# Attention and a gated feed-forward block in one kernel: the end of the program rebuilt, the order of TensorE's work written anew

## The reference

```python
q = (xn @ wq + bq)  # 16 heads of 16;  k, v: 2 groups of 16, each shared by 8 heads
q, k = rotary(q) * 16**-0.5, rotary(k)
attn = softmax(q k^T * 16**-0.5)            # per head, 1024 x 1024
x + (attn v) @ wo + bo + fwht(silu(xn @ W1.T) * (xn @ W3.T)) @ W2.T
```

## Time and profile before

| | us |
|---|---|
| three runs: lowest, median, highest | 1078.07, 1078.76, 1084.82 |
| the profiled execution: its time | 1075.6 |
| the profiled execution: span | 1073.8 |
| PE busy | 1014.3 (94%) |
| DVE busy | 771.2 (72%) |
| ACT busy | 707.5 (66%) |
| POOL busy | 347.2 (32%) |

### The profile page before, as it was taken

How to read it: one execution, slowest core, us unless ns; L and a number is a source line. 1 busy time by engine, 2 the same in 40 slices (tenths; PEclk the granted TensorE clock), 3 DMA queues, 4 the chain that set the end, 5 groups by cost and what they waited for, 6 DMA issues and landing times.

```text
span 1073.8 us, 19578 instructions
## 1 busy us (share of the span) xinstructions
PE 1014.3 (94%) x7604; PEld 549.6 (51%) x7604; DVE 771.2 (72%) x934; ACT 707.5 (66%) x1336; POOL 347.2 (32%) x300
## 2 busy tenths in 40 slices
PE   4889999999999999999999999999999999999997
PEld 3554445545554555545554455545555454644454
DVE  5996688677776778767786777767776778776723
ACT  4256677657765777657776577667775678566873
POOL 5262722073312634054310735126320224012300
PEclk9998999999999999999999999999999999999999
DMA  8762155212052253402242250521123131510001
GB/s 234 177 172 75 53 137 104 74 57 86 17 117 78 76 136 66 100 21 84 64 103 74 97 126 18 117 64 51 51 62 71 33 83 33 111 32 6 12 8 50
DMA packets 64941, 84.03 MB, mean 78 GB/s; under 512 B 19960, under 2 KB 34168, under 8 KB 64848
## 3 DMA queue, kind: packets, MB, share of 16 engines
q1 hardware_dynamic: 63296, 80.74, 29.1%
q10 hardware_dynamic: 1552, 2.03, 0.7%
HBM read 54.97 MB, written 22.51 MB: 72 GB/s over the span
## 4 chain that ended last, share of the span: by engine, by line
PE 66%; DVE 17%; ACT 5%; issue 4%; DMA 4%; SPq 3%; POOL 2%; DVEq 0%; ACTq 0%; POOLq 0%
PE ps L1501 16%; PE ps L1558 14%; PE ps L1545 13%; DVE negpart L1295 11%; PE ps L1456 9%; PE ps L1513 8%; PE ps L1467 3%; DVE hid L1267 3%; PE ps L1434 3%; ACT work L1079 2%; DMA qk_parts<-hid 1%; DMA xn<-in_x 1%; SPq L776 1%; SPq L784 1%; DMA recip_rows<-dens 1%
## 5 line engine op out<-in xcount | busy, mean ns | idle before, releaser
L1295 DVE TENSOR_REDUCE negpart<-ps 128x2 f32<-128x1024 f32 x512 | 619.0, 1224 | 235.7 <-PE ps L1456 234.8
L1079 ACT ACTIVATE work<-ps 128x512 f32<-128x512 f32 x1024 | 560.0, 603 | 262.3 <-PE ps L1545 256.9
L1558 PE MATMUL ps<-work,vb 128*32 128x512 f32 x2048 | 274.6, 609 | 5.8 <-ACT osum L1090 5.0
L1545 PE MATMUL ps<-qh,kb 50*128 50x512 f32 x1024 | 265.1, 450 | 10.3 <-ACT work L1079 7.4
L1456 PE MATMUL ps<-kb,qh 48*128 48x512 f32 x1024 | 226.8, 433 | 9.6 <-DVE negpart L1295 5.3
L1545 PEld LDWEIGHTS ps<-qh,kb 50*128 50x128 f32 x1024 | 123.4, 185 | 212.3 <-ACT work L1079 159.0
L1501 PE MATMUL ps<-xf,w_p 64*128 64x512 f32 x1536 | 218.3, 400 | 7.4 <-DVE negpart L1295 1.4
L1501 PEld LDWEIGHTS ps<-xf,w_p 64*128 64x128 f32 x1536 | 143.6, 185 | 49.7 <-DVE hid L1267 16.3
L933 POOL TENSOR_TENSOR hid_p<-hid,hid_p 128x512 fp32r<-128x512 f32 x64 | 82.2, 1286 | 203.1 <-ACT hid_p L1068 203.1
L1456 PEld LDWEIGHTS ps<-kb,qh 48*128 48x128 f32 x1024 | 98.1, 185 | 82.7 <-DVE negpart L1295 48.4
L1513 PEld LDWEIGHTS ps<-w2t_p,hid_p 64*128 64x128 f32 x1536 | 107.7, 185 | 34.2 <-DVE negpart L1295 27.1
(11 more groups left out here) (125 smaller groups left out, 484.6 us busy)
## 6 DMA issues: line engine op xcount, KB each, us to landing
xf<-xn_parts SPq DMA_DIRECT2D x32, 512.0 KB, 8.5
qh<-qk_parts SPq DMA_DIRECT2D x192, 64.0 KB, 2.3
xn_parts<-xt SPq DMA_DIRECT2D x14, 512.0 KB, 3.5
qh<-mturned SPq DMA_DIRECT2D x256, 2.0 KB
y<-in_x SPq DMA_DIRECT2D x8, 512.0 KB, 4.8
attnt<-osum SPq DMA_DIRECT2D x124, 32.0 KB, 2.0
recips<-recip_rows SPq DMA_DIRECT2D x120, 32.0 KB, 1.8
xn<-in_x SPq DMA_DIRECT2D x7, 512.0 KB, 5.0
```

The lines of the kernel that those rows point to most:

```text
L1079: nc.scalar.activation(prob[(ITSTEPS * i + j) % NPROB][:, h, :], ps[:, 4 + u % 3, :], ACT.Exp, scale=SCALE).then_inc(exp_done, 1)
L1295: nc.vector.tensor_reduce(negpart[a][:, f, :, h, t, e], two(slot), AX.X, ALU.max, negate=True).then_inc(ring_free[slot], 1)
L1545: pe.matmul(ps[:, 4 + u % 3, :], kb[i % 2][rows, kt * P:(kt + 1) * P], qh[2 * a + f][rows, h, :], start=True, stop=True).then_inc(s2_done, 1)
L1558: m = pe.matmul(ps[VW * h:VW * (h + 1), 7, :], vb[b % 2][g][:, kt, :], prob[(ITSTEPS * i + j) % NPROB][:, h, :], start=(kt == 0), stop=(kt ...
```

## The change

1. **The end.** The last iteration's output projection of half 0 moves from the closing into period 15 (kind `WOz`). To make room, the down products go one period sooner (11 to 14) and the last up product from period 10 to 9; VectorE's reciprocals of half 0 go from period 13 to 12.
2. **The closing.** VectorE turns the last sums straight from PSUM in blocks of 32 x 32, in two halves of 256 columns; in the turned layout each query's row sum stands beside its 16 values, so 8 reciprocals per partition do; it multiplies and turns back. Heads 4 to 7 then stand spread, 16 of each 32 partitions, so their output weights are loaded into `wo_last`, spread the same way with zeros between (a memset on GpSimd in iteration 6 and four DMAs on SyncE). TensorE adds the two parts of half 1 up in PSUM: first four matmuls over 64 partitions for heads 0 to 3, then four with `wo_last`. ScalarE's last copy, `select`, `chosen` and the wide reciprocals go.
3. **The orders.** On TensorE the kinds DN, WO, QK, None, WOx, QKx, UPxo, Nos and Not get another order, and WOo takes that of WO. On ScalarE most kinds get another order: copies of up products and projections come before an exponential that stood ahead of them, and where `osum` is saved the copy moves. UP and XT keep TensorE's order.

```diff
-    return range(4, 12) if i + 2 < NBLK else (1, 2, 3, 5, 6, 7, 8, 10)
+    return range(4, 12) if i + 2 < NBLK else (1, 2, 3, 5, 6, 7, 8, 10 if i + 1 < NIT else 9)
+def down_at(i):
+    return range(12, 16) if i + 1 < NIT else range(11, 15)
...
-    if p >= 12:
-        return ("DN", i, p - 12)
+    if i + 1 == NIT and p == PERIODS - 1:
+        return ("WO", i, 0)
+    if p in down_at(i):
+        return ("DN", i, down_at(i).index(p))
...
 # kind DN, TensorE
             sums_before()
+            scores(1)
             own(0)
-            scores(1)
             first(1)
...
-        elif kind == "WO":
+        elif kind in ("WO", "WOo"):
             scores(0)
             first(1)
+            scores(1)
             own(0)
-            scores(1)
             scores(2)
             first(1)
             own(1, 2, 3)
+            scores(3)
             first(1)
             sums_before()
             first(0)
             sums(i, 2 * p)
-            scores(3)
...
 # kind QK, TensorE
             own(1, 2, 3)
             first(1)
+            scores(3)
             sums(i, 2 * p)
-            scores(3)
             extra()
...
 # kind None, TensorE
             first(0)
+            sums(i, 2 * p)
             first(1)
             scores(3)
-            sums(i, 2 * p)
...
+        elif kind == "WOx":
+            scores(0)
+            first(1)
+            own(0, 1)
+            first(1)
+            own(2, 3)
+            scores(1)
+            first(1)
+            sums_before()
+            sums(i, 2 * p)
+            first(0)
+            scores(2)
             extra()
             scores(3)
...
-        elif kind == "WOo":
-            first(0)
-            sums_before()
-            first(0)
-            first(1)
-            scores(0)
-            scores(1)
-            own(0, 1, 2, 3)
-            scores(2)
-            sums(i, 2 * p)
-            first(1)
-            scores(3)
...
-        elif kind == "DNz":
+        elif kind == "WOz":
             scores(0)
             scores(1)
+            sums_before()
             scores(2)
-            own(0)
+            own(0, 1)
             scores(3)
-            own(1, 2)
-            sums_before()
+            own(2, 3)
             sums(i, 2 * p)
-            own(3)
...
 # SyncE, iteration i, ahead of move_sums(i, 1)
+                if i == NIT - 2:
+                    sp.wait_ge(wo_zero, 1)
+                    for h in range(QUAD):
+                        at = (NG - 1) * P + (QUAD + h) * HD
+                        sp.dma_start(wo_last[VW * h:VW * h + HD, :], wo[at:at + HD, :]).then_inc(wo_last_in, 16)
...
 # ScalarE, kind UP
                         gate(i, up_at(i).index(p))
-                        exponentials(i, j, 5, 6)
                         linear(i, up_at(i).index(p))
-                        exponentials(i, j, 6, 8)
+                        exponentials(i, j, 5, 8)
 # ScalarE, kind QK
                         exponentials(i, j, 0, 5)
                         projected(i + 2, 0)
-                        exponentials(i, j, 5, 6)
                         projected(i + 2, 1)
-                        exponentials(i, j, 6, 8)
+                        exponentials(i, j, 5, 7)
                         projected(i + 2, 2)
+                        exponentials(i, j, 7, 8)
 # ScalarE, kind WOo
-                        exponentials(i, j, 0, 5)
+                        exponentials(i, j, 0, 7)
+                        hidden_before(i, p)
                         save_finished(i, p)
-                        exponentials(i, j, 5, 8)
-                        hidden_before(i, p)
+                        exponentials(i, j, 7, 8)
...
 # VectorE, the closing
+            dve.wait_ge(pv_done, ITSTEPS * NIT)
+            for n, cols in enumerate(halves):
+                nc.vector.transpose(last_sums[:, cols], ps[:, 7, cols]).then_inc(last_turned, 1)
             for n in range(2):
-                cols = slice(n * 2 * P, (n + 1) * 2 * P)
-                dve.wait_ge(last_turned, 1)
-                nc.vector.reciprocal(last[GRP:P, cols], ps[GRP:P, 5, cols]).then_inc(last_recip, 1)
-                dve.wait_ge(last_turned, 2)
-                dve.wait_ge(last_recip, n + 2)
-                nc.vector.tensor_tensor(attnt[GRP:P, 1, cols], ps[GRP:P, 4, cols], last[GRP:P, cols],
-                                        ALU.mult).then_inc(last_norm, 1)
-            projected_sums(NIT - 1, 0)
+                dve.wait_ge(last_turned, n + 1)
+                nc.vector.reciprocal(shares[n], blocks[n][:, :, HD]).then_inc(last_step, 1)
             for n in range(2):
-                at = y[:, (NBLK - 1) % 2, 2 * n:2 * n + 2, :].rearrange("p t d -> p (t d)")
-                dve.wait_ge(*filled(("WO", NIT - 1, 1), n + 1))
-                nc.vector.tensor_tensor(at, at, two(0)[:, n, :], ALU.add).then_inc(ring_free[0], 1)
+                dve.wait_ge(last_step, n + 1)
+                nc.vector.tensor_tensor(blocks[n][:, :, 0:HD], blocks[n][:, :, 0:HD],
+                                        shares[n].unsqueeze(2).broadcast_to([P, 2 * P // VW, HD]), ALU.mult).then_inc(last_step, 1)
+            for n, cols in enumerate(halves):
+                dve.wait_ge(last_step, n + 3)
+                nc.vector.transpose(last_attn[:, cols], last_sums[:, cols]).then_inc(last_norm, 1)
+            for n in range(2):
+                dve.wait_ge(last_full, n + 1)
+                at = y[:, (NBLK - 1) % 2, 2 * n:2 * n + 2, :]
+                nc.vector.tensor_tensor(at, at, ps[:, 2 * n + 2:2 * n + 4, 0:D], ALU.add).then_inc(last_added, 1)
...
 # TensorE, the closing, after the last sums
-                pe.wait_ge(osum_done, 4 * NIT)
-                pe.wait_ge(chosen_set, 2)
-                for n in range(2):
-                    pe.matmul(ps[GRP:P, 5 - n, :], chosen[:, n, :], osum[:, :], start=True, stop=True).then_inc(last_turned, 1)
+                pe.wait_ge(norm_done, 2 * NIT)
+                for k in range(BT):
+                    bank = ps[:, 2 + k, 0:D]
+                    pe.matmul(bank, attnt[0:GRP, 1, k * P:(k + 1) * P], wo_sb[0:GRP, NG - 1, :], start=True, stop=False)
+                pe.wait_ge(wo_last_in, 16 * QUAD)
+                for k in range(BT):
+                    pe.wait_ge(last_norm, k // 2 + 1)
+                    bank = ps[:, 2 + k, 0:D]
+                    m = pe.matmul(bank, last_attn[:, k * P:(k + 1) * P], wo_last, start=False, stop=True)
+                    if k % 2 == 1:
+                        m.then_inc(last_full, 1)
```

More of the change, by code:

```diff
@@ L279, in walk_iteration @@
             scores(1)
+            first(1)
             sums_before()
-            first(1)
-            own(1)
             scores(2)
             scores(3)
+            own(1)
             first(1)
@@ L342, in walk_opening, with walk_closing @@
         piece(("UP", 0, c), k, 2 + c % 2)
-def walk_closing(sums, piece, select):
+def walk_closing(sums, piece, last_values):
     sums(NIT - 1, ITSTEPS - 1)
-    select()
-    for half in range(QB):
-        for k in range(4):
-            piece(("WO", NIT - 1, half), k, 1 - half)
+    last_values()
 def ring_table():
@@ L459, in build @@
         last = qe[1][:, :]
+        last_sums, last_attn = (prob[1][:, n, :] for n in range(2))
+        last_dens = prob[1][:, 2, 0:512 // VW]
+        wo_last = tabq_sb[:, 0, 0:D]
         rot_b1 = [attnt[:, n, :] for n in range(2)]
@@ L545, in build @@
         norm_done = sem("norm_done")
[L546 removed]
+        wo_zero = sem("wo_zero")
+        wo_last_in = sem("wo_last_in")
         last_in = sem("last_in")
@@ L1005, in _ @@
                         normalise_sums(i, 0)
+                    if p == 0 and i == NIT - 2:
+                        nc.gpsimd.memset(wo_last, 0.0).then_inc(wo_zero, 1)
             pool.wait_ge(moved[1], N_MOVE * (2 * NIT - 1))
@@ L1402, in _ @@
                         gated(i, up_at(i).index(p))
-                    elif kind == "DNz":
-                        down(i, p - 12)
+                    elif kind == "WOz":
+                        projected_sums(*main_entry(i, p)[1:])
                     if p == 1 and i > 0:
@@ L1573, in _ @@
                 walk_iteration(i, score, sums, piece)
-            walk_closing(sums, piece, select)
+            walk_closing(sums, piece, last_values)
 def kernel(**inputs):
```

76 lines of the change are left out of this document (34 added, 42 removed).

## The result

| | before | after |
|---|---|---|
| median, us | 1080.84 (20 runs, 1075.61 to 1087.52) | 1087.73 (20 runs, 1083.1 to 1094.04) |
| ratio, 95% interval | | 1.0062 [1.0041, 1.0083] |
| profiled execution: span, mean granted clock | 1073.8, 0.990 | 1090.3, 0.969 |

What follows compares the result with a forecast made beforehand. TensorE's list was taken to set the pace. Terms -4.1 + 0.1 - 2.5 - 1.3 - 0.8 - 3.1 - 1.5 - 1.0 + 0.25 = -13.95 took 1078.76 to 1064.8 us; range 1055 to 1076.

Steps and rivals of the forecast that it cites:

- an order can only give back what it wastes: Whole kernel: TensorE's list sets the pace; waste is idle time and time between starts of matmuls that count as busy.
- in places where it now stands: Sign of being wrong: the clock falls at places where it held before; no size given.
- WOo as WO: WOo in WO's order: -2.5 us at period 0, -1.3 at period 4 with a GpSimd wait, -0.8 for half a clock fall.
- Down periods: First look after a down quarter, not a score pair: 0.11 us in each of 28, -3.1; lower bound nothing.
- WOx, None, WO, QK: New orders of these periods: WOx -1.5 us, None -1.0, QK with the next WO +0.25.
- Opening kinds: First two periods, 17.88 us at clock 0.62: new order worth 0, bounds -5 and +3.
- The closing: From the last sums' end to the span's end: 8.5 us instead of 12.55, -4.1, bounds -5.5 and -2.3.
- The last iteration before it: Last iteration's periods from 9 to the last sums: +1.6 and, in period 15, -1.0 and -0.46; together 0.1, bounds -1 and +1.5.
- Only the end counts: Rival, 27%: moved pieces change which wait shows, not the sum; -4.0, -2.5 and 0.5 for the rest stay: 1071.8 us.
- The clock no longer falls in the opening: Rival, 14%: the opening's low-clock stretch goes, worth 4 to 5 us more: 1060 us.
- ScalarE's list becomes the wait: Rival, 9%: a copy ahead of exponential 5 costs 0.3 us in each of 59 up periods, +17.7: 1082 us.

Runs made afterwards that it cites:

- e5_fill_wo: The changed kernel with extra matmuls, results overwritten, in TensorE's pauses: two in WO, six in WOo at period 0, four at period 4; 1079.41 us, ratio 0.9982.
- the end alone: The kernel before with parts 1 and 2 of the change only, all orders as before; 1073.45 us (ratio 0.9921), run again 1071.04 (0.9904).
- e2_orders: The kernel before with part 3 of the change, the new orders, alone and the end as before; 1095.82 us, ratio 1.0113.
- e8_end_dn: The kernel before with parts 1 and 2 and, of the new orders, only that of the down periods; 1073.55 us, ratio 0.9926.
- e4_wo_back: The changed kernel with WO, WOo and QK in their orders of before, on TensorE and ScalarE; 1084.32 us, ratio 1.0022.
- e9_best: The changed kernel with Nos, Not, QKx, UPxo, None and ScalarE's DNo orders as before, plus e5_fill_wo's extra matmuls; 1072.98 us, ratio 0.9919.
- e12_best_open: e9_best with five more extra matmuls ahead of the opening's first look; 1069.24 us, ratio 0.9889 against the kernel before.

## Why the prediction was wrong, by its steps

**The step that failed is "an order can only give back what it wastes", read as idle time and starts at one clock.** The prediction priced each order by idle time that goes, and took the clock as given but for one fall and a rival. Moving the same pieces left as many pauses, at other places, and the clock went with them: e5_fill_wo gives 8.3 us back by filling those of WO and WOo and nothing else. Of the 20.9 us between forecast and result about 8 are the clock's, 20 us more at the lower level at 0.41. The rest is that the orders gave nothing at one clock: forecast at -10.0 together, they cost 1 to 3 us, which is the changed kernel's own time (-2.6) less that of the end alone (-5.8, and -3.8 when run again), and +1.9 in e2_orders. The last sentence on what would make it wrong, falls "in places where it now stands", is what happened. The profile of before showed what a fall costs, 1.64 us for one WOo; no chance was given to more of them, though the rival on the opening said that the wait of the new WOo could bring one.

**WOo as WO: -2.5 and -1.3 forecast, -0.8 for the fall.** The step that failed here asked only what the new order needs from GpSimd; it didn't ask what scores at the first place of an iteration need. They wait for the row maxima by DMA, in the period before: at full clock 17.01 against 16.95 for the pair of periods in iteration 7, and in iteration 6, where the wait was 2.22, 9.76 + 8.04 = 17.80 if its WOo had kept the full clock: so +0.1 and +0.85 where -1.27 each was forecast. At period 4 the wait for GpSimd was seen, but the period took 9.34, not 8.95: the wait for GpSimd is 0.7 of its 1.5 us of idle, the rest is waits for ScalarE and VectorE that the prediction had left out. That is -0.25 each. The fall at (7,4) stayed.

**Down periods: -3.1 forecast, 0 measured**, in the changed kernel (7.46) and in e8_end_dn (7.47). The lower bound in the prediction named the reason, that VectorE's freeing of the slot ends last anyway: the first look is 0.34 us long still and idle for 0.08 on that wait. The gain between two starts was no gain, since the slot wasn't free at the earlier one.

**WOx, None, WO, QK: -2.25 forecast.** WOx gave 0.21 in each of five, -1.0 (-1.5 forecast); QK 10.67 to 10.47, and WO +0.13, so -0.35 for +0.25. None was better than thought in itself, 0.3 to 0.7 each, but the DNo behind one in iteration 6 lost 0.85 (1.7 in all, if the one in iteration 0 lost as much), and a DNo in between went from 8.34 to 8.49. Opening kinds had 0 with +3 as a bound; with them back the own time is 0.8 lower and the lower level 4 us shorter. These terms don't add up to the 1 to 3 us that the orders cost at one clock; where the rest lies stays open.

**The closing: -4.1 forecast, -5.1 measured.** The mechanism and the order of its steps were right; mis-sized were the reciprocals (0.16 each where 0.2 was taken), the products (0.23, not 0.3) and above all what follows the last add, 2.7 us instead of 3.5. The turn was taken right at 0.41: it is 0.39. The estimate by the Trainium skill, "VectorE: DVE Perf Modes", "The three transpose paths", was 0.46, a little long; the bound of 0.70 was far off. **The last iteration before it: +0.1 forecast, -0.7 measured**, 45.95 us from period 9 to the last sums' end against 46.63. The output product of half 0 and VectorE's add were hidden in period 15 as said; None cost 4.63 us instead of 6.0, and the down period behind it 7.31, as its scores wait.

**The rivals.** "Only the end counts" was right about the first look and the bank, and about DN and WOo at period 4, but it kept WOo at period 0 and didn't know of the clock. That its 1071.8 is near the end alone (1073.45, 1071.04) is chance: 2.5 of its 7 us were to come from WOo. "The clock no longer falls in the opening" was the opposite of what came. "ScalarE's list becomes the wait" didn't happen: UP is 7.59 as before. The side that slower got 7% came by a mechanism that the prediction mentioned under another rival, and priced nowhere.

**What stays open.** Why the opening's clock falls in each profile with the new orders of WOx and UP (but for the one with the pause filled), though nothing of those kinds runs before it; that filling the pause takes it away shows the pause as its condition, not what differs between the kernels. Why, for the same pause of 0.59 us, three WO of five have the fall and two have not. And why the profile of after has falls of 3.4 and 10.2 us in the first iteration, at 115.6 and 129.2, that those of e4_wo_back and e5_fill_wo have not, though nothing differs between them there.

## What to carry to other kernels

Where TensorE is busy nearly all the time (94% here), look at each pause's place and length before an order is changed, and at the granted clock of every stretch after: where the clock fell beside it, a pause of 0.59 us cost 1.55 us more. A period's order can't be priced by itself; price it with the period before and the one behind, and ask what its new first piece waits for. Where a pause can't be ordered away, matmuls whose result is overwritten are worth a trial, in a bank that is free at that point and in none that others must free first.

## What the runs showed of the hardware

- The clock fell beside pauses of 0.59 us in an otherwise full period: WO at 0.82 took 9.67 us, at full clock 8.12, so 1.55 for a pause of 0.59. It did so in 10 of 20 such WO; with two matmuls in the pause in none of 15 (e5_fill_wo, e9_best, e12_best_open).
- The time at the lower level differs from run to run of one kernel: 19.3 to 54.3 us over 24 runs of the kernel before. At 0.36 to 0.41 us each that is up to 14 us between two runs, and a comparison of two single profiles of such kernels is one of two clocks as well.
- On VectorE a turn in 32 x 32 blocks of 128 x 256 four-byte elements took 0.39 us out of PSUM and 0.38 out of SBUF, about as long as an add of that size (0.41).
